# Stage 1's long convolution turned round: input stationary in 32-column tiles, Toeplitz tiles moving; x loaded in two parts, output stored by units

## The chip, the cores and the metric

The kernel runs on one core of a Trainium2 chip. The metric is device time in microseconds of one execution, input load and output store included. The engines are PE (TensorE; PEld is its weight load), DVE (VectorE), ACT (ScalarE), POOL (GpSimd) and SP (SyncE), which here only issues DMAs.

## The reference

A decoder of four layers, each with self attention, cross attention and a feed-forward part, on x of shape (32, 128, 128): 32 sequences, 128 steps, 128 channels, all float32. Every one of the twelve stages ends in `x = layernorm(x + stage(x))`. The stage that the change is in is the first cross attention. Cut to what matters:

```python
# per sequence b: h = layernorm(x) * g + b; sparse attention over ctx (best 32 of 128 keys) gives c
# film = c @ W_film + b_film: scale and shift for the way in and the way out
u  = h * film_in_scale + film_in_shift
# long convolution along the 128 steps, one kernel K[d, :] of 128 taps per channel d
y  = irfft(rfft(u, 2L) * rfft(K, 2L))[:L] + u * D_skip
x1 = x + y * film_out_scale + film_out_shift
out = x + layernorm(x1 + mlp(layernorm(x1))) * g + b
```

## The kernel before

x stays in SBUF as `X` (128 steps on the partitions, 32 sequences, 128 channels) from the first stage to the last. Each stage is a program for all engines, written by hand with semaphores; a stage consists of one or more blocks, and all engines meet at the end of each block. The weights of a stage are fetched while the stage before runs, into one of two large tiles that take turns.

**Start and end.** `load_stage` issues four DMAs from SP in this order: constants, weights of stage 0, x (L365), ctxT (L366). DVE makes small constants and then waits for all of x, and no engine leaves the block before the others. `store_stage` is a block of its own after the last stage: one DMA of X to the output (L400), and a wait for it. In stage 11 (`experts_gelu`) ACT writes X by units of 4 sequences (`block_out`, L4629), each announced by `x_out`.

**Stage 1 (`film_conv`), front block.** Eight units of 4 sequences, on all engines. DVE does the selection of the best 32 keys in four rounds r: `best(u, r, g)` (8 largest, L2838) and `replaced(u, r, g)` (L2855), each for half g of a unit. Between these stand `shifted(u)` (L2873, needs POOL's `root(u)`), `inverse(u-1)` (L2879, needs ACT's sums of exponentials `denominators(u-1)`, L2746), `weights(u-1)` (L2885, needs `inverse`), and `kernel_taps(u)`. POOL's order in a unit u is `root(u)` (L2668, L2671), `chosen(u-1)` (L2681 and L2686, four times; the first waits for `weights(u-1)`), `modulated(u-1)` (L2695 to L2702; L2700 waits for ACT's `film` of L2789 and L2790), then the products for the convolution kernel (L2655, L2660). ACT's `rest(u-1)` (L2758) waits for POOL's L2686 from the third sequence of a unit on, and `exponentials`, `normed` and `filmed` come behind it. The channels' taps gather in `kz`, which SP stores to DRAM (`s4d_kernel`, L2646) once `kernel_sb` is up, some 30 us before the block ends.

**Stage 1, convolution block.** For each channel d the 128 x 128 Toeplitz matrix of its taps is read from `s4d_kernel` by overlapping rows, 16 channels (1024 KB) in a chunk, eight chunks, two buffers: chunk c is issued (L3033) when chunk c-2 has been used. PE does one matmul a channel (L3058): the Toeplitz tile is stationary, and the 32 columns of `UY` (that channel of all 32 sequences) move. DVE (L3047) and ACT (L3039) take turns to copy a chunk's 512 results a partition back into `UY`. All four engines run this as a loop of four steps.

**Stage 1, back block** (L3088 on): SP fetches stage 2's weights; the MLP and the norms follow; its first instruction on DVE reads `UY`.

Matmuls of float32 stand in the trace as two records each, with two weight loads; a transpose as one.

## Time and profile before

| what | value |
|---|---|
| median of 3 runs | 3392.13 us (3390.64 to 3396.54) |
| the profiled execution's own time, and its span | 3384.0 us, 3382.2 us |
| busy over the span: PE, PEld, DVE, ACT, POOL | 82%, 58%, 57%, 41%, 39% |
| granted TensorE clock, mean | 0.889 of full |
| front block of stage 1 | about us 300 to 631.7 |
| convolution block | 631.7 to 693.4 |
| back block | 693.4 to 812 |

The granted clock of TensorE has two levels, 1.2 and 2.4 GHz, shown as 0.50 and 1.00. A row of a timeline has the start, the length, the engine with its line, the operation and, in brackets, how long the engine was idle before and what released it. Busy shares are means over twelve stages with different limits, so what an edit is worth has to be read in its own stretch.

### The profile page before, as it was taken

Reading aid. Unit: us, or ns where it says so; the run is one execution under the profiler, and the core shown is the slowest. Engines: PE = TensorE matmul, PEld = TensorE weight load, DVE = VectorE, ACT = ScalarE, POOL = GpSimd, SP = SyncE. Lnnn points to the kernel's source line nnn. Section 1 sums busy time; section 2 is a strip of 40 time slices with the busy share of each in tenths; the row PEclk is TensorE's granted clock in tenths of the full one; section 3 lists DMA queues with packets and bytes.
Section 4 is the critical chain, followed back from the end, with each engine's and each line's share of the span. In section 5 each row is a group of like instructions: output and inputs, shape, how many; then the busy total and the mean of one; then the engine's idle time right before and its main releaser. Section 6 shows DMA issues by size and latency. Waiting matters only on the chain. (4 is left out here: it accounts for less than half of the span.)

```text
span 3382.2 us, 78574 instructions
## 1 busy us (share of the span) xinstructions
PE 2764.0 (82%) x31778; PEld 1972.8 (58%) x31785; DVE 1936.9 (57%) x5109; ACT 1387.2 (41%) x3112; POOL 1326.2 (39%) x1389
## 2 busy tenths in 40 slices
PE   6992666776665999799899986998789999978985
PEld 3551343654443777566799975666366666655665
DVE  5997998044555344466454444564855555545665
ACT  3552565244344555344322213553143344434554
POOL 3542565154311111444233333453733333324555
PEclk9996777578677999899899997997999999998998
DMA  3000000300000000100000000001000000000000
GB/s 101 3 2 1 1 1 1 87 24 1 1 7 32 1 2 2 40 3 3 8 1 1 1 1 16 2 2 42 4 2 2 2 2 2 2 5 6 2 2 26
DMA packets 24453, 37.29 MB, mean 11 GB/s; under 512 B 568, under 2 KB 21184, under 8 KB 23232
## 3 DMA queue, kind: packets, MB, share of 16 engines
q1 hardware_dynamic: 24096, 32.30, 3.0%
q8 instruction: 253, 4.15, 0.5%
q14 instruction: 104, 0.85, 0.1%
HBM read 30.07 MB, written 2.23 MB: 10 GB/s over the span
## 5 line engine op out<-in xcount | busy, mean ns | idle before, releaser
L1193 POOL TENSOR_TENSOR L_attn__qk<-L_attn__turned 128x512 f32<-128x512 f32 x128 | 161.3, 1271 | 353.0 <-DVE L_attn__turned L1302 353.0
L4247 PE MATMUL psum<-L_ffn__e_hT,weights 128*128 128x256 f32 x1024 | 244.8, 383 | 0.0
L777 DVE TENSOR_REDUCE L_xattn__nm<-psum 128x8 bf16<-128x1024 f32 x128 | 156.4, 1224 | 149.4 <-PE psum L970 143.1
L1302 DVE TENSOR_TENSOR L_attn__turned<-psum,weights 128x1024 f32<-128x1024 f32 x128 | 153.4, 1219 | 144.6 <-PE psum L1409 141.7
L4247 PEld LDWEIGHTS psum<-L_ffn__e_hT,weights 128*128 128x128 f32 x1024 | 186.8, 192 | 20.7
L4101 DVE TENSOR_TENSOR L_ffn__e_a<-L_ffn__e_sg,psum 128x512 f32<-128x512 f32 x128 | 88.0, 687 | 176.5 <-ACT L_ffn__e_sg L4093 176.4
L4093 ACT ACTIVATE L_ffn__e_sg<-psum 128x512 f32<-128x512 f32 x128 | 76.4, 597 | 258.9 <-PE psum L4247 258.9
L717 ACT ACTIVATE L_xattn__pT<-psum 128x1024 f32<-128x1024 f32 x128 | 124.0, 1021 | 59.0 <-PE psum L998 59.0
L4260 PEld LDWEIGHTS psum<-weights,L_ffn__e_a 128*128 128x128 f32 x1024 | 134.4, 191 | 7.2 <-DVE L_ffn__e_a L4101 0.7
L1409 PE MATMUL psum<-L_attn__xT,weights 128*128 128x256 f32 x512 | 136.2, 399 | 2.0 <-DVE L_attn__turned L1302 1.3
L4260 PE MATMUL psum<-weights,L_ffn__e_a 128*128 128x128 f32 x1024 | 135.0, 275 | 0.5 <-DVE L_ffn__e_a L4101 0.5
L1239 ACT ACTIVATE L_attn__qk<-L_attn__qk 128x512 bf16<-128x512 f32 x128 | 77.4, 631 | 87.1 <-POOL L_attn__qk L1193 87.1
L777 DVE TENSOR_REDUCE L_ffn__nm<-psum 128x8 bf16<-128x1024 f32 x64 | 78.2, 1224 | 56.3 <-PE psum L970 56.3
L4020 POOL TENSOR_TENSOR L_ffn__e_half<-L_ffn__e_prod 128x512 f32<-128x512 f32 x32 | 40.6, 1267 | 171.7 <-DVE L_ffn__e_prod L4110 171.7
L712 ACT ACTIVATE L_attn__pT<-L_attn__pT,L_attn__sc 128x1024 f32<-128x1024 f32 x64 | 72.9, 1148 | 79.0 <-DVE L_attn__pT L787 79.0
L1409 PEld LDWEIGHTS psum<-L_attn__xT,weights 128*128 128x128 f32 x512 | 90.4, 192 | 24.1 <-issue 9.7
L2855 DVE MATCH_REPLACE8 L_xattn__front_left<-L_xattn__front_top,L_xattn__front_left 128x128 f32<-128x128 f32 x384 | 101.2, 284 | 0.0
L1627 POOL TENSOR_TENSOR L_xattn__rstd<-L_xattn__mv,eps 128x2 f32<-128x2 f32 x16 | 3.1, 194 | 237.4 <-DVE L_xattn__mv L1749 237.4
L1262 ACT ACTIVATE L_attn__pT<-psum 128x1024 f32<-128x1024 f32 x64 | 62.0, 1021 | 72.7 <-PE psum L1470 72.7
L1311 DVE TENSOR_REDUCE L_attn__nm<-psum 128x8 bf16<-128x1024 f32 x64 | 75.4, 1220 | 26.5 <-PE psum L1440 25.8
L777 DVE TENSOR_REDUCE L_attn__nm<-psum 128x8 bf16<-128x1024 f32 x64 | 77.9, 1220 | 19.1 <-PE psum L970 19.1
L2973 PE MATMUL psum<-L_xattn__front_diag,L_xattn__front_ex 128*128 128x128 f32 x256 | 58.2, 399 | 35.9 <-POOL L_xattn__front_ex L2686 35.9
(669 smaller groups left out, 7649.8 us busy)
## 6 DMA issues: line engine op xcount, KB each, us to landing
L_xattn__toeplitz<-s4d_kernel SPq DMA_DIRECT2D x8, 1024.0 KB, 5.6
weights<-pack SPq DMA_DIRECT2D x1, 3328.0 KB, 11.1
weights<-pack SPq DMA_DIRECT2D x1, 3140.0 KB, 10.4
weights<-pack SPq DMA_DIRECT2D x1, 2370.0 KB, 9.0
out_dram<-X SPq DMA_DIRECT2D x1, 2048.0 KB, 8.7
weights<-pack SPq DMA_DIRECT2D x1, 1732.5 KB, 10.3
ctxT<-ctxT_in SPq DMA_DIRECT2D x1, 1536.0 KB, 21.7
weights<-pack SPq DMA_DIRECT2D x1, 1376.0 KB, 5.8
```

What stands on the lines that cost most here:

```text
L717: nc.scalar.activation(unit, scores[u], ACT.Exp, scale=scale).then_inc(p_sb, 1)
L777: nc.vector.tensor_reduce(nm[:, n % 2, :].rearrange("p (g c) -> p g c", g=4)[:, 2 * u:2 * u + 2, 0:4], scores[u].rearrange("p g (i q) -> p ...
L1193: nc.gpsimd.tensor_tensor(qk[:, p % 2, u], turned[:, g % 2, :, 0:2 * P], turned[:, g % 2, :, 2 * P:4 * P], ALU.add).then_inc(qk_sb, 1)
L1239: nc.scalar.activation(qk16[:, p % 2, u], qk[:, p % 2, u], ACT.Copy).then_inc(qk16_sb, 1)
L1302: nc.vector.tensor_tensor(turned[:, g % 2], proj[u % 2].unsqueeze(1).to_broadcast([P, 2, 4 * P]), k.w(name + "rope").rearrange("p (t q) -> ...
L1311: nc.vector.tensor_reduce(nm[:, n % 2, :].rearrange("p (g c) -> p g c", g=4)[:, 2 * u:2 * u + 2, 0:4], scores[u].rearrange("p g (j q) -> p ...
L1409: last = nc.tensor.matmul(proj[place % 2][:, 2 * P * t:2 * P * t + 2 * P], w[:, P * c:P * c + P], xT[:, p % 2, :], start=True, stop=True)
L2855: last = nc.vector.match_replace(left[:, u % 2, j, h, :], top[:, u % 2, j, h, 8 * r:8 * r + 8], source(u, r, j, h), 2 * NEG)
L4093: nc.scalar.activation(sg[:, g % 2, :], gate[g % 2], ACT.Silu).then_inc(sg_sb, 1)
L4101: nc.vector.tensor_tensor(a[:, g % 2].rearrange("p c s q -> p (c s q)"), sg[:, g % 2, :], up[g % 2], ALU.mult).then_inc(a_sb, 1)
L4247: last = nc.tensor.matmul(bank[g % 2][:, 256 * c:256 * c + 256], k.w(name + w)[:, o:o + P], hT, start=True, stop=True)
L4260: last = nc.tensor.matmul(Y[s][e // 4][:, P * (e % 4):P * (e % 4) + P], a[:, g % 2, c, s, :], k.w(name + "Wd")[:, P * (2 * e + c):P * (2 * ...
```

## The change

Five edits:

1. **Convolution.** The 32 columns of `UY` of a channel become the stationary operand and the Toeplitz tile (128 columns) moves. Four channels at a time use the four 32-column tiles of the array and write to four groups of 32 partitions of one bank. The result stands turned (sequence on the partitions), so ACT copies it to `turned`, PE transposes it back in four transposes a chunk, and DVE copies it into `UY`. The loops are written out.
2. **Chunks.** All eight chunks get their own buffers. The first three go into the weights' tile that is not in use, and are issued in the front block, right after `s4d_kernel` has been stored and POOL's last product has been made. The other five are issued at the start of the convolution block without waits.
3. **DVE's order in the front.** `inverse(u-1)` moves from the end of round 0 to after both halves of `best` in round 1; `weights(u-1)` moves from between these two halves to after `replaced(u, 1, 0)` and `shifted(u)`.
4. **x in two parts.** Sequences 0 to 7, then 8 to 31, with a semaphore each. Stage 0 starts after the first; PE and POOL wait for the second ahead of pair 4.
5. **Output by units.** SP stores each unit of 4 sequences (256 KB) in stage 11 as soon as `x_out` says so; `store_stage` only waits.

```diff
@@ load_stage
-            sp.dma_start(k.X[:], k.x.rearrange("b t d -> t b d")).then_inc(k.x_loaded, 16)
+            xs = k.x.rearrange("b t d -> t b d")
+            sp.dma_start(k.X[:, 0:8, :], xs[:, 0:8, :]).then_inc(k.x_loaded, 16)
+            sp.dma_start(k.X[:, 8:NB, :], xs[:, 8:NB, :]).then_inc(k.x_rest, 16)
             sp.dma_start(k.ctxT[:], k.ctxT_dram).then_inc(k.ctx_loaded, 16)
@@ film_conv, front, SP
                         sp.wait_ge(kernel_stored.sem, 16)
+                        sp.wait_ge(kdiff_sb, COARSE)
+                        for c in range(AHEAD):
+                            sp.dma_start(ahead[:, c], tiles[:, CH * c:CH * c + CH, :]).then_inc(toe_in[c], 16)
@@ film_conv, front, DVE
                                 best(u, r, 0)
+                                best(u, r, 1)
                                 if r == 1 and u >= 1:
-                                    weights(u - 1)
-                                best(u, r, 1)
+                                    inverse(u - 1)
...
                                 replaced(u, r, 0)
                                 if r == 1:
                                     shifted(u)
+                                    if u >= 1:
+                                        weights(u - 1)
                                 replaced(u, r, 1)
-                                if r == 0 and u >= 1:
-                                    inverse(u - 1)
@@ film_conv, convolution block (new)
+                @block.sync
+                    for c in range(AHEAD, CHUNKS):
+                        sp.dma_start(taps_of(c), tiles[:, CH * c:CH * c + CH, :]).then_inc(toe_in[c], 16)
+                @block.scalar
+                    for c in range(CHUNKS):
+                        act.wait_ge(conv_ps, c + 1)
+                        if c >= 2:
+                            act.wait_ge(back_ps, c - 1)
+                        nc.scalar.activation(turned[:, c % 2, :], C_bank[c % 2], ACT.Copy).then_inc(conv_sb, 1)
+                @block.vector
+                    for c in range(CHUNKS):
+                        dve.wait_ge(back_ps, c + 1)
+                        nc.vector.tensor_copy(UY[:, :, CH * c:CH * c + CH],
+                                              T_bank[c % 2].rearrange("p (d b) -> p b d", b=NB)).then_inc(back_sb, 1)
+                @block.tensor
+                    def convolve(c):
+                        pe.wait_ge(toe_in[c], 16)
+                        if c >= 2:
+                            pe.wait_ge(conv_sb, c - 1)
+                        taps = taps_of(c)
+                        for g in range(CH // 4):
+                            for q in range(4):
+                                d = 4 * g + q
+                                last = nc.tensor.matmul(C_bank[c % 2][32 * q:32 * q + 32, P * g:P * g + P],
+                                                        UY[:, :, CH * c + d], taps[:, d, :], start=True, stop=True,
+                                                        skip_group_check=True)
+                        last.then_inc(conv_ps, 1)
+                    def turn_back(c):
+                        pe.wait_ge(conv_sb, c + 1)
+                        if c >= 2:
+                            pe.wait_ge(back_sb, c - 1)
+                        for g in range(CH // 4):
+                            last = nc.tensor.transpose(T_bank[c % 2][:, P * g:P * g + P],
+                                                       turned[:, c % 2, P * g:P * g + P], k.w("ident"))
+                        last.then_inc(back_ps, 1)
+                    convolve(0)
+                    for c in range(CHUNKS):
+                        if c + 1 < CHUNKS:
+                            convolve(c + 1)
+                        turn_back(c)
@@ experts_gelu, SP
-                k.load_weights(sp, k.next_stage(stage))
+                for u in range(UNITS):
+                    sp.wait_ge(x_out, u + 1)
+                    sp.dma_start(k.out.rearrange("b t d -> t b d")[:, 4 * u:4 * u + 4, :],
+                                 k.X[:, 4 * u:4 * u + 4, :]).then_inc(k.stored, 16)
```

Stage 11 had no next stage, so the line removed there issued nothing. In stage 0, `if stage == 0 and p == 4` puts a wait for `x_rest` ahead of POOL's `with_bias(4)` and PE's transposes of pair 4.

## Rows read from the trace of the kernel before

**Rows 1.** The convolution: busy time of engines, granted clock, DMA share, GB/s:

```profile
632.00:693.40 61.40, 54.81 (x256) 54.69 (x256) 2.77 (x4) 2.39 (x4) 0.00 (x0) 0.50 0.48 137
```

**Rows 2.** PE and ACT over the convolution, in order of time:

```profile
637.84 54.81 PE L3058 MATMUL psum<-L_xattn__UY,L_xattn__toeplitz 128*128 x256 [6.77 <-DMA L_xattn__toeplitz<-s4d_kernel]
692.79 0.60 ACT L3039 ACTIVATE L_xattn__UY<-psum 128x512 f32 x1 [13.06 <-PE psum L3058]
```

**Rows 3.** The timeline of SP's queue, us 590 to 700:

```profile
599.22 0.34 SPq L2646 DMA_DIRECT2D s4d_kernel<-L_xattn__kz  x1
631.96 47.44 SPq L3033 DMA_DIRECT2D L_xattn__toeplitz<-s4d_kernel  x8
```

**Rows 4.** The Toeplitz transfers issued in us 600 to 660:

```profile
DMA to landing us min/median/max: 5.4/5.6/8.8
```

**Rows 5.** PE's timeline in stage 0, 32-column tiles, and one window's clock:

```profile
45.04 1.94 PE L1012 MATMUL psum<-L_attn__pT,L_attn__vz 128*32 128x128 f32 x32
52.70 1.08 PE L1012 MATMUL psum<-L_attn__pT,L_attn__vz 128*32 128x128 f32 x32
...
45.04:46.98 1.94, 1.94 (x42) 1.47 (x40) 1.23 (x1) 1.45 (x2) 0.00 (x0) 0.50 0.00 0
```

**Rows 6.** PE's timeline in the front of stage 1, full array:

```profile
484.73 1.06 PE L2924 MATMUL psum<-consts,X 128*128 128x128 f32 x4
495.80 2.04 PE L2973 MATMUL psum<-L_xattn__front_diag,L_xattn__front_ex 128*128 128x128 f32 x8 [0.87 <-POOL L_xattn__front_ex L2686]
```

**Rows 7.** The timeline of SP's queue at the start:

```profile
1.79 0.83 SPq L365 DMA_DIRECT2D X<-x_in  x1
2.67 10.94 SPq L366 DMA_DIRECT2D ctxT<-ctxT_in  x1
```

**Rows 8.** The timeline of POOL at the start of stage 0:

```profile
18.06 0.31 POOL L611 MEMSET L_attn__nm<- 128x256 bf16 x1 [15.44 <-POOLq L359]
```

**Rows 9.** DMA issues: KB each, us from issue to landing:

```profile
out_dram<-X SPq DMA_DIRECT2D x1, 2048.0 KB, 8.7
weights<-pack SPq DMA_DIRECT2D x1, 321.5 KB, 2.9
s4d_kernel<-L_xattn__kz SPq DMA_DIRECT2D x1, 128.0 KB, 2.1
X<-x_in SPq DMA_DIRECT2D x1, 0.5 KB, 15.7
```

**Rows 10.** The timeline at the end:

```profile
3373.10 0.39 SPq L400 DMA_DIRECT2D out_dram<-X  x1
```

**Rows 11.** Timelines of ACT, DVE and POOL in unit 6 of the front:

```profile
517.05 0.38 ACT L2790 ACTIVATE L_xattn__FO<-psum 128x256 f32<-128x256 f32 x1
...
522.32 0.25 DVE L2879 RECIPROCAL L_xattn__front_den<-L_xattn__front_den 128x16 f32<-128x16 f32 x1 [2.97 <-ACT L_xattn__front_etop L2746]
524.05 0.76 DVE L2885 TENSOR_TENSOR L_xattn__front_den<-L_xattn__front_den,L_xattn__text_gate 128x16 f32<-128x16 f32 x1
...
527.51 1.02 POOL L2671 TENSOR_TENSOR L_xattn__front_rstd<-L_xattn__front_rstd,neg_half 128x4 f32<-128x4 f32 x1
528.50 1.04 POOL L2681 TENSOR_TENSOR L_xattn__front_diag<-consts,L_xattn__front_den 128x512 f32<-128x512 f32 x1
```

**Rows 12.** Timelines of DVE and POOL, units 0 and 1 of the front:

```profile
317.22 0.17 DVE L2873 SCALAR_TENSOR_TENSOR L_xattn__front_shift<-L_xattn__front_mv,L_xattn__front_rstd 128x4 f32<-128x4 f32 x1
...
349.96 0.92 DVE L2873 SCALAR_TENSOR_TENSOR L_xattn__front_shift<-L_xattn__front_mv,L_xattn__front_rstd 128x4 f32<-128x4 f32 x1
...
340.52 1.01 POOL L2671 TENSOR_TENSOR L_xattn__front_rstd<-L_xattn__front_rstd,neg_half 128x4 f32<-128x4 f32 x1
346.38 1.04 POOL L2681 TENSOR_TENSOR L_xattn__front_diag<-consts,L_xattn__front_den 128x512 f32<-128x512 f32 x1 [4.85 <-DVE L_xattn__front_den L2885]
```

**Rows 13.** Waits in the front: engine, line, releaser; total us, times, longest:

```profile
DVE L_xattn__front_den L2879 <- ACT L_xattn__front_etop L2746: 23.5, 6, 13.4
POOL L_xattn__front_diag L2681 <- DVE L_xattn__front_den L2885: 7.5, 2, 4.9
```

More of the change, by code:

```diff
@@ L399, in _ @@
         def _(sp):
-            sp.dma_start(k.out.rearrange("b t d -> t b d"), k.X[:]).then_inc(k.stored, 16)
-            sp.wait_ge(k.stored, 16)
+            if 11 in STAGES:
+                sp.wait_ge(k.stored, 16 * (NB // 4))
+            else:
+                sp.dma_start(k.out.rearrange("b t d -> t b d"), k.X[:]).then_inc(k.stored, 16)
+                sp.wait_ge(k.stored, 16)
 def rms_root(k, pool, ms, s, t, mean_square, plus_eps, root):
@@ L563, in with_bias @@
                 def with_bias(p):
+                    if stage == 0 and p == 4:
+                        pool.wait_ge(k.x_rest, 16)
                     if p >= 2:
@@ L902, in turn @@
                         pe.wait_ge(xT_sb, p)
+                    if stage == 0 and p == 4:
+                        pe.wait_ge(k.x_rest, 16)
                     for s in range(2):
@@ L2450, in film_conv @@
         kernel_stored = sig.one("kernel_stored", 16, 1)
+        CH, AHEAD = 16, 3
+        CHUNKS = P // CH
+        tiles = bass.AP(tensor=kernel_dram, offset=0, ap=[[1, P], [2 * P, P], [1, P]])
+        toe_in = [sig.one(f"toeplitz_loaded{c}", 16, 1).sem for c in range(CHUNKS)]
+        ahead = k.weights[1 - BUFFER[stage]][:, 0:AHEAD * CH * P].rearrange("p (c d l) -> p c d l", c=AHEAD, d=CH)
         with ExitStack() as mid:
@@ L3017, in film_conv, with sb, event, taps_of @@
         with ExitStack() as ctx:
-            CH = 16
-            toeplitz = ctx.enter_context(nc.sbuf_tensor(f"{name}_toeplitz", [P, 2, CH, P], F32))
-            toe_in = sig.pair("toeplitz_loaded", 16)
-            conv_ps, conv_sb = sig.pair("conv_ps"), sig.pair("conv_sb")
-            tiles = bass.AP(tensor=kernel_dram, offset=0, ap=[[1, P], [2 * P, P], [1, P]])
+            def sb(what, shape, dt=F32):
+                return ctx.enter_context(nc.sbuf_tensor(f"{name}_conv_{what}", shape, dt))
+            def event(what):
+                return sig.one("conv_" + what, 1, 1).sem
+            toeplitz = sb("toeplitz", [P, CHUNKS - AHEAD, CH, P])
+            turned = sb("turned", [P, 2, 4 * P])
+            C_bank, T_bank = k.bank[0:2], k.bank[2:4]
+            conv_ps, conv_sb, back_ps, back_sb = event("ps"), event("sb"), event("back_ps"), event("back_sb")
+            def taps_of(c):
+                return ahead[:, c] if c < AHEAD else toeplitz[:, c - AHEAD]
             with nc.Block() as block:
@@ L3028, in _ @@
                 def _(sp):
-                    for c in range(P // CH):
-                        s, turn_of = c % 2, c // 2
-                        if turn_of:
-                            sp.wait_ge(conv_ps[s].sem, turn_of)
-                        sp.dma_start(toeplitz[:, s], tiles[:, CH * c:CH * c + CH, :]).then_inc(toe_in[s].sem, 16)
+                    for c in range(AHEAD, CHUNKS):
+                        sp.dma_start(taps_of(c), tiles[:, CH * c:CH * c + CH, :]).then_inc(toe_in[c], 16)
@@ L3035, in _ @@
                 @block.scalar
                 def _(act):
-                    with act.Fori(0, P // (2 * CH)) as t:
-                        act.wait_ge(conv_ps[1].sem, conv_ps[1].at(t, 1))
-                        nc.scalar.activation(UY[:, :, bass.ds(2 * CH * t + CH, CH)],
-                                             k.bank[5][:].rearrange("p (d b) -> p b d", b=NB),
-                                             ACT.Copy).then_inc(conv_sb[1].sem, 1)
+                    for c in range(CHUNKS):
[3 more added lines that the diff above has]
+                        nc.scalar.activation(turned[:, c % 2, :], C_bank[c % 2], ACT.Copy).then_inc(conv_sb, 1)
@@ L3051, in _ @@
                 @block.tensor
                 def _(pe):
-                    with pe.Fori(0, P // (2 * CH)) as t:
-                        for s in range(2):
-                            pe.wait_ge(toe_in[s].sem, toe_in[s].at(t, 16))
-                            pe.wait_ge(conv_sb[s].sem, conv_sb[s].at(t, 0))
-                            for j in range(CH):
-                                last = nc.tensor.matmul(k.bank[4 * s + 1][:, NB * j:NB * j + NB], toeplitz[:, s, j, :],
-                                                        UY[:, :, bass.ds(2 * CH * t + (CH * s + j), 1)], start=True,
-                                                        stop=True)
-                            last.then_inc(conv_ps[s].sem, 1)
+                    def convolve(c):
[10 more added lines that the diff above has]
+                        last.then_inc(conv_ps, 1)
```

8 lines of the change are left out of this document (3 added, 5 removed).

## The prediction, made before the changed kernel was run

> **What bounds the kernel now.** I read the page first, only to see that no single engine bounds it: PE is busy 82% of the span, DVE 57%, and these are means over twelve stages. An edit is therefore worth what it is worth in its own stretch, and I went to five: the start, the front of stage 1, its convolution, the block behind it and the end.
>
> In the convolution PE itself is the limit: 54.8 us busy out of 61.4, at half clock (0.50) all the while, with the DMA share below half [rows 1]. The reader should see the order of time as well: PE waits 6.8 us for its first chunk, then never again, and ACT's last copy ends at 692.79 + 0.60 = 693.4 [rows 2]. SP's queue is empty between 599.22 and 631.96, when the chunks are issued [rows 3]. At the start every engine stands until 18.06 [rows 8], because x, issued at 1.79, lands 15.7 us later, at 17.5 [rows 7, 9]. At the end one store of 2048 KB takes 8.7 us with nothing beside it [rows 9, 10].
>
> The front needs the most care, since the edit of DVE's order is made there. DVE looks like the victim of a wait: it waits 23.5 us in six places for ACT's sums before `inverse` [rows 13]. But follow unit 6. ACT's film ends at 517.4; POOL then adds the film, makes the products and the root, and ends the root at 527.51 + 1.02 = 528.53. Its `chosen` starts at 528.50, at once. DVE had finished `weights` at 524.05 + 0.76 = 524.8, 3.7 us earlier [rows 11]. POOL waited for DVE there in two units only, 7.5 us together [rows 13]: the second (unit 1) and the last. So the round trip POOL, ACT, PE, ACT, POOL sets the pace of the front, DVE follows it, and DVE's wait is slack.
>
> **The change part by part.**
>
> *Convolution.* The same form of matmul, a 32-column tile with 128 float32 columns moving, stands in stage 0: 32 records took 1.94 us at half clock (0.50) and 1.08 us in a later instance, which I take for the full level [rows 5]. A chunk is 16 channels of two records, so 32 records, against 54.8 / 8 = 6.85 us now [rows 1]. Four full transposes are added to each chunk, 1.06 us [rows 6]. A chunk then costs PE 2.1 to 3.0 us, eight cost 17 to 24. The copies (0.60 us each on ACT [rows 2], about as much on DVE) run beside it, and only the last shows.
>
> The rate of chunks is the other limit. Of the two issued together at 631.96 the first landed after 5.6 us, at 637.6, the later one 8.8 us after its own issue, some 0.36 us later, so at 641.1 [rows 3, 4]: 3.5 us a chunk. Three chunks are fetched in the empty time of the queue, from about 601.4 (599.22 + 2.1 [rows 3, 9]): 5.6 + 2 x 3.5 = 12.6 us, there by 614. The waits put on SP are met: nothing else is queued on it, and POOL's last product is long made. The other five are issued at 631.96 and the last lands at 637.6 + 4 x 3.5 = 651.6. PE starts it at 651.8 (it started 0.2 us after landing before [rows 2]); + 1.08 for the chunk, + 0.60 for ACT's copy, under which the transposes of chunk 6 lie, + 1.06, + 0.7 for DVE's copy and 0.3 for hand-overs = 655.5. Saved: 693.4 - 655.5 = 37.9 us. If PE stays at half clock, it is the bound from 632.1 on: 24 + 0.7 = 656.8, saved 36.6. I take 37.9, since two limits meet at nearly the same time.
>
> One rule speaks against this price. The Trainium skill, "TensorE: Matmul & The Clock Gate", Part 3, The mechanism, says that a weight load overlaps a running matmul only where their row groups differ, and four column tiles all use every row. By its figure of columns / 1.2 ns, 27 ns for 32 columns, an estimate is 0.86 us more for 32 records, on the path once, behind the last landing: 37.0 saved. The trace speaks against it, because rows 5 have 32 loads and 32 matmuls in 1.08 us.
>
> *DVE's order.* What it adds is told by POOL's first instruction of `chosen(u-1)`. Before, `weights(u-1)` was ready before the root in units 2 to 7. Now it stands behind `shifted(u)`, which needs the very root that POOL does just ahead of `chosen`. So POOL ends the root, DVE does `shifted` (0.17 us when POOL is idle [rows 12]) and `weights` (about the same), and only then POOL goes on: about 0.45 us with hand-overs, six times = 2.7 us. If the two ran as long as they do beside a busy POOL (0.92 and 0.76 [rows 11, 12]) it would be 1.8, six times = 10.8. I take 0.45, as POOL is waiting, not working. Behind it on POOL stand all of `chosen` and `modulated`; ACT's `rest`, `exponentials` and film wait for these, and so the loop that sets the pace. Unit 1 is dearer: DVE is late there, POOL already waits until 346.38 with its root done at 341.5, and `shifted` comes at 349.96 [rows 12]. `weights` will come right behind it, at about 350.15, and POOL starts at 350.4: + 4.1. The last `weights` keeps its place. The removed wait (23.5 - 13.4 = 10.1 us in five places [rows 13]) only moves to `shifted`, where DVE now waits for the root. Sum: + 6.8 us, bounds + 14.9 (4.1 + 10.8) and, if DVE did set the pace, - 10.1.
>
> *x in two parts.* The last three quarters of x, 1536 KB, take 5.3 us at 3.5 us per 1024 KB, so sequences 0 to 7 are there by 12.2 instead of 17.5. But nobody leaves the block before SP, and SP sits in the issue of ctxT until 2.67 + 10.94 = 13.6 [rows 7]; the order and bytes in the queue stay the same. The block ended 0.57 us after the last event before (17.5 to 18.06). New start: 14.2, - 3.9 us. Bounds: - 5.3, if SP gets free as early as x, and 0, if it is held until all of x is down. The waits for the rest, ahead of pair 4, cost nothing: in 17.5 us it is down, while stage 0 is at its first pairs. On SP one more issue of 0.8 us lies under the blocked one.
>
> *Output by units.* Seven stores lie under the work of the units behind them. The last one, 256 KB, lies between 128 KB in 2.1 us and 321.5 KB in 2.9 us [rows 9]; I take 2.7 for 8.7: - 6.0 us, bounds - 6.6 and - 5.8.
>
> *Elsewhere* nothing moves: the back block's weights are fetched in its own block as before, and the tile borrowed for three chunks is free by then.
>
> **Sum.** - 37.9 + 6.8 - 3.9 - 6.0 = - 41.0 us. The profiled execution took 3384.0 us around a span of 3382.2, so it would take 3343.0. It was 8.1 us quicker than the median of the runs, which I take for a property of the profiled execution and not of the work. Predicted median: 3392.1 - 41.0 = 3351.1 us. Differences under 0.2%, 6.8 us, I count as none.
>
> **The rivals.**
>
> *The front pays nothing, or gains.* If units overlap so that POOL's later start is made good by an earlier DVE, the 6.8 go away: 3344.3. If DVE's waits were the pace, 10.1 us come off as well: 3334.2. For it: in unit 1 DVE is late, and POOL waits 4.85 us for it [rows 12]. Against it: POOL's 3.7 us of distance in unit 6, and only two waits of POOL for DVE.
>
> *The change doesn't do what it says: the three early chunks don't come early*, because SP is held at one of its waits until the block's end. Then eight chunks follow each other from 631.96: 637.6 + 7 x 3.5 = 662.1, + 3.9 for the same tail = 666.0, saved 27.4, time 3361.6. Against it: 30 us of empty queue. The same time comes out if transfers run at two thirds of the rate measured.
>
> *The column tiles don't run beside each other in the array*, and the kernel is slower. Each record then costs what one in the full array costs, 2.04 / 8 = 0.255 us [rows 6]: 8.2 us a chunk, 9.2 with the transposes, 632.1 + 8 x 9.2 + 0.7 = 706.4, + 13.0 for the convolution in place of - 37.9, in all + 9.9: 3402.0. It decides the sign from about 7.8 us a chunk of matmuls: (61.4 + 9.7 - 0.8) / 8 - 1.06. Against it: 1.94 at half clock for the same count [rows 5]. What is new is that the weights are read with a stride of 512 bytes.
>
> **How the numbers follow.** The forecast (chunks set the pace, the front pays) has 0.50; the front paying nothing or gaining 0.27; chunks late or slow 0.15; tiles one after another 0.04; 0.04 for several small misses that leave 10 us or less. The likeliest case alone has 3346 to 3360, from its bounds. The range reaches from the front with most of its gain to late chunks with the front's price a little higher: 3336 to 3366. Only the third rival, and part of the last case, are not faster: faster 0.94, same 0.02, slower 0.04.
>
> **What would show it.** In the profile after: stage 0 starts at about 14 instead of 18.06; in SP's queue three Toeplitz issues at about 601 and five at the start of the block; PE's groups of 32 records in 1.1 to 1.9 us, and waits of PE for DMA between the later chunks; the convolution block about 23.5 us long; DVE's wait at `inverse` gone and one at `shifted` in its place; POOL waiting for `weights` in every unit, 4 us in unit 1 and about half a microsecond in the others; the last store under 3 us. The prediction is wrong if POOL's waits are nearly nil, if the front gets shorter, if PE's granted clock in the front shifts (the five units from 346.38 to 528.50 took 36.4 us each [rows 11, 12], and 3% of that, over six units, is already the price that I put on the front), or if PE doesn't reach the pace of the transfers.

## The result, and the profile after

The changed kernel took 3347.56 us (median of 4 runs, 3341.05 to 3352.58) beside 3392.94 us for the kernel before on the same chip (4 runs, 3390.64 to 3396.54): ratio 0.9869, interval 0.9854 to 0.9884, that is 44.5 us less (39 to 50). A second timing of the same two kernels gave 3352.83 us beside 3391.37: ratio 0.9881, interval 0.9866 to 0.9896. The two medians lie 3.5 us under and 1.7 us over the predicted 3351.1.

The span of the profiled execution went from 3382.2 to 3343.4 us. I cut both at the same instructions:

| stretch | before, us | after, us | difference | predicted |
|---|---|---|---|---|
| start, until POOL's first record of stage 0 | 18.06 | 14.14 | -3.9 | -3.9 |
| stage 0, until the root of unit 0 of the front | 289.9 | 288.4 | -1.5 | 0 |
| to the root of unit 1 | 32.5 | 32.5 | 0 | 0 |
| front: root of unit 1 to the convolution's Toeplitz issue | 291.4 | 299.3 | +7.9 | +6.8 |
| convolution: that issue to the first record of the block behind | 61.7 | 25.1 | -36.6 | -37.9 |
| that block and stages 2 to 11, until the last write of X starts | 2677.5 | 2679.6 | +2.1 | 0 |
| from there to the end of the span | 11.0 | 4.4 | -6.6 | -6.0 |
| sum | 3382.2 | 3343.4 | -38.8 | -41.0 |

**The convolution.** PE's timeline of the changed kernel over the block (start, duration, in brackets the idle time before it and what ended it), which answers to [rows 2]:

```profile
634.43 3.73 PE L3084 MATMUL psum<-weights,L_xattn__UY 128*32 128x128 f32 x64 [0.94 <-PEq L2658]
638.09 1.11 PE L3094 MATMUL psum<-consts,L_xattn__conv_turned 128*128 128x128 f32 x4
639.14 1.41 PE L3084 MATMUL psum<-weights,L_xattn__UY 128*32 128x128 f32 x32
...
641.06 1.26 PE L3084 MATMUL psum<-L_xattn__conv_toeplitz,L_xattn__UY 128*32 128x128 f32 x32
642.25 0.66 PE L3094 MATMUL psum<-consts,L_xattn__conv_turned 128*128 128x128 f32 x4
643.68 1.25 PE L3084 MATMUL psum<-L_xattn__conv_toeplitz,L_xattn__UY 128*32 128x128 f32 x32 [0.77 <-DMA L_xattn__conv_toeplitz<-s4d_kernel]
...
648.44 1.25 PE L3084 MATMUL psum<-L_xattn__conv_toeplitz,L_xattn__UY 128*32 128x128 f32 x32 [2.92 <-DMA L_xattn__conv_toeplitz<-s4d_kernel]
...
652.05 2.02 PE L3084 MATMUL psum<-L_xattn__conv_toeplitz,L_xattn__UY 128*32 128x128 f32 x32 [1.51 <-DMA L_xattn__conv_toeplitz<-s4d_kernel]
...
655.29 1.80 PE L3084 MATMUL psum<-L_xattn__conv_toeplitz,L_xattn__UY 128*32 128x128 f32 x32 [0.17 <-DMA L_xattn__conv_toeplitz<-s4d_kernel]
657.02 1.41 PE L3094 MATMUL psum<-consts,L_xattn__conv_turned 128*128 128x128 f32 x8
```

The first four chunks find their tiles there, and the last four wait for a transfer (the very last for 0.17 us only): transfers bound the end of the block, not PE. Read the durations too: 1.87 us for 32 records in the first pair, 1.25 in the middle, 2.02 near the end. The granted clock of the same stretches goes with them (columns: window, length, busy time and count on PE, weight loads, DVE, ACT, POOL, then the granted clock, DMA share and GB/s):

```profile
634.40:638.20 3.80, 3.77 (x65) 3.41 (x66) 0.00 (x0) 0.62 (x1) 0.00 (x0) 0.50 0.67 190
639.10:644.90 5.80, 5.03 (x106) 4.13 (x105) 2.08 (x3) 1.36 (x2) 0.00 (x0) 0.95 1.15 301
644.90:648.40 3.50, 0.62 (x6) 0.38 (x4) 0.69 (x1) 0.60 (x1) 0.00 (x0) 1.00 1.19 292
652.00:655.30 3.30, 3.08 (x38) 2.29 (x38) 0.14 (x1) 0.60 (x1) 0.00 (x0) 0.50 0.56 137
```

The granted clock is at the half level (0.50) at first and nearly at the full one (0.95) after. While PE stands idle for the transfers, from 645.5 to 648.4, it is still 1.00, and it is 0.50 under the chunk that starts at 652.05.

**SP's queue** answers to [rows 3 and 7]; the first four lines are the start, the others the surroundings of the convolution:

```profile
1.63 0.43 SPq L367 DMA_DIRECT2D X<-x_in  x1
2.28 3.66 SPq L368 DMA_DIRECT2D X<-x_in  x1
5.98 7.75 SPq L369 DMA_DIRECT2D ctxT<-ctxT_in  x1
14.14 0.35 SPq L350 DMA_DIRECT2D weights<-pack  x1
...
605.75 0.34 SPq L2663 DMA_DIRECT2D s4d_kernel<-L_xattn__kz  x1
608.03 5.45 SPq L2667 DMA_DIRECT2D weights<-s4d_kernel  x3
634.39 13.67 SPq L3057 DMA_DIRECT2D L_xattn__conv_toeplitz<-s4d_kernel  x5
```

SP is free of ctxT's issue at 5.98 + 7.75 = 13.73, and stage 0 starts 0.4 us later, at 14.14, as was worked out. The three early chunks are issued 26 us before the block, and have landed before it starts.

**The front.** POOL's and DVE's waits in the front of the changed kernel (engine, line, releaser; us in total, times, longest), beside [rows 13]:

```profile
POOL L_xattn__front_xg L2720 <- ACT L_xattn__FO L2810: 117.6, 8, 16.9
POOL L_xattn__front_diag L2701 <- DVE L_xattn__front_den L2905: 13.6, 8, 8.7
...
DVE L_xattn__front_shift L2893 <- POOL L_xattn__front_rstd L2691: 23.7, 6, 4.2
DVE L_xattn__front_den L2899 <- ACT L_xattn__front_etop L2766: 20.5, 7, 15.0
```

POOL now waits for the weights in every unit, 13.6 us instead of 7.5. DVE waits 23.7 us at `shifted` for POOL, where it did not wait before. Its wait at `inverse` is not gone: the one of the last unit is still there (13.4 us before, 15.0 now), and of the other 10.1 us 5.5 are left, in six places. So DVE stands idle some 20 us more in all; the price is what POOL waits, not this. The hand-over in unit 3, on POOL and DVE:

```profile
420.40 1.02 POOL L2691 TENSOR_TENSOR L_xattn__front_rstd<-L_xattn__front_rstd,neg_half 128x4 f32<-128x4 f32 x1
421.78 1.04 POOL L2701 TENSOR_TENSOR L_xattn__front_diag<-consts,L_xattn__front_den 128x512 f32<-128x512 f32 x1 [0.37 <-DVE L_xattn__front_den L2905]
...
421.45 0.16 DVE L2893 SCALAR_TENSOR_TENSOR L_xattn__front_shift<-L_xattn__front_mv,L_xattn__front_rstd 128x4 f32<-128x4 f32 x1 [3.91 <-POOL L_xattn__front_rstd L2691]
421.53 0.17 DVE L2905 TENSOR_TENSOR L_xattn__front_den<-L_xattn__front_den,L_xattn__text_gate 128x16 f32<-128x16 f32 x1
```

POOL's root ends at 421.42, `shifted` starts at 421.45, `weights` follows, and POOL's `chosen` starts at 421.78.

**The end.** The last write of X, whose four records end at 3340.69, then nothing but the last store (2.7 us to the end of the span, 3343.4):

```profile
3339.04 1.65 ACT L4673 ACTIVATE X<-L_ffn__r,L_ffn__shift,L_ffn__rstd 128x128 f32<-128x128 f32 x4 [4.21 <-DVE L_ffn__shift L4753]
```

### The profile page after: what moved, and what is told of

The parts are those of the page before. It is cut to its first block and busy times, and to the rows that moved or that the text cites. A ratio compares the mean times of both kernels' runs of the same rounds, so it can differ in the third digit from the quotient of the medians.

```text
span 3343.4 us, 78491 instructions
## 1 busy us (share of the span) xinstructions
PE 2724.1 (81%) x31810; PEld 1931.3 (58%) x31817; DVE 1930.9 (58%) x5113; ACT 1390.3 (42%) x3116; POOL 1326.8 (40%) x1389
## 5 line engine op out<-in xcount | busy, mean ns | idle before, releaser
L722 ACT ACTIVATE L_attn__pT<-L_attn__pT,L_attn__sc 128x1024 f32<-128x1024 f32 x64 | 72.9, 1149 | 79.1 <-DVE L_attn__pT L797 79.1
## 6 DMA issues: line engine op xcount, KB each, us to landing
weights<-pack SPq DMA_DIRECT2D x1, 3328.0 KB, 10.5
```

## The experiments

Each kernel is the changed one with one edit, unless it says otherwise. Ratios are against the kernel before, run on the same chip; its own median lay between 3388.17 and 3392.94 us from timing to timing, so kernels of different timings are compared by their ratios. "Front" below is the stretch from the root of unit 1 to the first Toeplitz issue of the convolution block, and "later stages" is that from the block behind the convolution to the last write of X.

### The old order of DVE's operations

```
 best(u, r, 0)
-best(u, r, 1)
 if r == 1 and u >= 1:
-    inverse(u - 1)
+    weights(u - 1)
+best(u, r, 1)
...
 shifted(u)
-if u >= 1:
-    weights(u - 1)
 replaced(u, r, 1)
+if r == 0 and u >= 1:
+    inverse(u - 1)
```

> The changed kernel with DVE's order in the front of stage 1 put back (inverse at the end of round 0, weights between the two halves of best in round 1). My theory: the loop through POOL and ACT sets the pace, so POOL's new waits (3.8 us more in unit 1, 0.37 us in six units) go away and the span falls by 6.1 us from 3343.4 to about 3337, give or take 5 for the granted clock; POOL waits for weights in two units only, as before. Rival: DVE's wait for the sums is what costs, then taking the new order away makes the front 10 us longer, span 3353.

Measured: 3347.4 us, ratio 0.9884 (0.9865 to 0.9903). In the trace POOL waits for weights in two units again (4.86 and 2.69 us), and the front takes 289.8 us instead of 299.3: 9.5 us less. But the later stages took 2689.7 us instead of 2679.6, the span is 3342.4 us where some 3337 were expected, and the ratio, beside 0.9869, shows no gain. The place of the price is confirmed, its worth for the whole kernel is not; it was run again further down.

### The new order alone, in the kernel before

The same edit in the other direction, made to the kernel before.

> The kernel before with only the new order of the VectorE operations. Theory: the wait of GpSimd for the weights of unit 0 grows from 4.9 to 8.7 us, and in the six later units one of 0.4 us appears; from the second root to the first Toeplitz issue of the convolution it takes 297 to 300 us instead of 291.4, so the kernel is 5 to 9 us slower than before. Rival: the order costs only the 3.8 us of unit 1, and the rest of the changed kernel's 7.9 us came from its other parts (the Toeplitz chunks fetched ahead, granted clock): 295 us, 4 us slower.

Measured: 3398.70 us beside 3390.33 (12 and 17 runs), ratio 1.0020 (1.0009 to 1.0031): 6.8 us slower (3 to 10.5). POOL's waits for weights are the 13.6 us in 8 places of the changed kernel:

```profile
POOL L_xattn__front_diag L2681 <- DVE L_xattn__front_den L2885: 13.6, 8, 8.7
```

The front took 296.2 us in the profiled execution, 4.8 more than before. That is between what the two theories gave, and the median is in the range of both. What is settled: with this order alone the kernel before is slower, and the waits are all there. Where the 6.8 us lie is not settled: in this profiled execution the later stages took 2687.3 us against 2677.5, which is more than the front lost.

### The products one place earlier on POOL

If POOL sets the pace, then work that stands between the film and `chosen` on POOL should come off when it is moved under POOL's wait for the film.

```
 pool.wait_ge(u2_sb, u + 1)
+if u + 2 < COARSE:
+    kernel_products(u + 2)
 pool.wait_ge(film_sb, 4 * u + 4)
...
 if u == 0:
     kernel_products(0)
-if u + 1 < COARSE:
-    kernel_products(u + 1)
+    kernel_products(1)
```

> The changed kernel with POOL's products for the convolution kernel (7.1 us a unit) moved to where POOL waits for ACT's film, so that they no longer stand between the film and the next root. My theory, that the loop over POOL sets the pace: the loop loses 7.1 of its 37.9 us, and DVE, busy some 33.5 us a unit, becomes the pace, so 4 us in each of six units go, about 24 us, span about 3320 (3317 to 3328). Rival, DVE or ACT with PE set the pace: nothing changes, span 3340 to 3346.

Measured: 3332.47 us, ratio 0.9832 (0.9813 to 0.9851). The front took 288.6 us, 10.7 less than in the changed kernel, where 24 were expected. The waits say where the rest went:

```profile
POOL L_xattn__front_xg L2722 <- ACT L_xattn__FO L2811: 75.3, 8, 16.3
POOL L_xattn__front_diag L2701 <- DVE L_xattn__front_den L2906: 32.6, 8, 8.7
```

POOL's wait for the film fell by 42 us, and 19 us of that came back as a wait for DVE's weights, 3.5 us in each of the six middle units, which was 0.37 before. So POOL's work between the film and `chosen` did lie on the loop that sets the pace (POOL itself is busy for only 22 us of a unit), and 7 us a unit taken off it bring up the next limits. Which they are, the units show (a unit counted from POOL's first `chosen` to the next one; columns as above). The first two lines are this run, the third is a unit of the kernel with the early weights, described next:

```profile
452.15:489.87 37.72, 25.16 (x108) 14.40 (x107) 32.95 (x222) 21.84 (x83) 22.24 (x18) 0.73 0.00 1
489.87:523.87 34.00, 22.76 (x108) 13.43 (x107) 32.84 (x222) 21.85 (x83) 22.25 (x18) 0.80 0.00 1
444.39:478.39 34.00, 22.77 (x105) 13.49 (x106) 34.00 (x222) 21.78 (x84) 22.25 (x17) 0.80 0.00 1
```

Four of the six units took 34.0 to 35.3 us. The other two kept 37.7: the granted clock in them is 0.73, and DVE waits for PE. In a unit of 34.0 us DVE is busy for 32.8 and waits 1.2 for ACT's sums, while POOL waits for DVE; in the third line DVE is busy for all of the 34.0, and is the limit. And in this run the stretch behind the last `chosen` took 32.8 us against 28.7 in the changed kernel's, which no part of the edit explains.

### The old order and the early products together

The two edits above, and, in the second kernel, `inverse(0)` and `weights(0)` moved right behind `statistics(1)`:

```
 statistics(u)
+if r == 0 and u == 1:
+    inverse(0)
+    weights(0)
```

> The old order with the kernel products early, without the early weights of unit 0. If the early weights in unit 1 made the 12.9 us by which the mixed kernel's front was shorter than that of the early products alone, this front takes some 284 us or more; if the old order did it together with the early products, it takes 279 to 281 us (the mixed kernel's 275.7 plus the 4 to 5 us of unit 1).

> The changed kernel with three edits to the front: the old order of the VectorE operations back, the kernel products of the next unit moved ahead of the film add on GpSimd, and, in unit 1 alone, the inverse and the weights of unit 0 right after the statistics of unit 1. Theory (GpSimd's chain sets the front until VectorE's own 33 us a unit do): the first diagonal product of unit 1 starts 10 us after the second root instead of 4 us later still, the wait for the first weights falls from 4.9 to under 1 us, the periods of the units are the 34.0 us (or 37.6 us at the lower granted clock) of the run with the products early, and the stretch from the second root to the first Toeplitz issue of the late block is some 284 us instead of 299; the median some 12 to 16 us under the changed kernel. Rival: VectorE is the limit already in both, and the old order gives nothing on top of the early products: 288 us for the stretch, and the median of the run with the early products alone.

Measured: without the early weights of unit 0 3336.13 us, ratio 0.9828 (0.9814 to 0.9842), front 284.1 us; with them 3331.18 us, ratio 0.9827 (0.9808 to 0.9846), front 275.7 us. Between the front of the early products alone (288.6) and that of the mix lie 12.9 us, 4.5 of them on the step to the old order and 8.4 on the step to the early weights; the first theory had some 284 us or more for the kernel between. Of these, POOL's wait in unit 1 accounts for 3.8 and 4.9 us (8.68, then 4.86, then nothing); the rest is within what fronts of one order vary. On POOL, unit 1 of the mix starts `chosen` straight behind the root, where it waited 8.68 us in the changed kernel:

```profile
336.89 1.01 POOL L2691 TENSOR_TENSOR L_xattn__front_rstd<-L_xattn__front_rstd,neg_half 128x4 f32<-128x4 f32 x1
337.86 1.04 POOL L2701 TENSOR_TENSOR L_xattn__front_diag<-consts,L_xattn__front_den 128x512 f32<-128x512 f32 x1
```

The ratios of all three kernels with early products lie within 0.0005 of each other, so what the front gains on top of the early products isn't resolved by the timings. Each of the three is some 0.4 to 0.5% under the changed kernel: of the two timed side by side, 0.9828 (0.9814 to 0.9842) against 0.9881 (0.9866 to 0.9896).

### All chunks issued in the block

```
-sp.wait_ge(kdiff_sb, COARSE)
-for c in range(AHEAD):
-    sp.dma_start(ahead[:, c], ...)
...
-for c in range(AHEAD, CHUNKS):
+for c in range(CHUNKS):
```

> The changed kernel with all eight Toeplitz chunks issued at the start of the convolution block, none in the front. If the pace of the chunks bounds the block (3.5 us each), the block grows by three chunks, 10.5 us, from 25.0 to about 35.5, span about 3354. Rival, PE bounds it and the early fetch only hides the first landing: the block grows by no more than the wait for the first chunk, 5 to 6 us, span about 3349.

Measured: 3362.2 us, ratio 0.9922 (0.9901 to 0.9943). SP's queue and a part of PE's timeline:

```profile
631.99 5.50 SPq L3054 DMA_DIRECT2D weights<-s4d_kernel  x3
637.53 19.01 SPq L3054 DMA_DIRECT2D L_xattn__conv_toeplitz<-s4d_kernel  x5
667.70 0.35 SPq L350 DMA_DIRECT2D weights<-pack  x1
...
637.86 2.00 PE L3081 MATMUL psum<-weights,L_xattn__UY 128*32 128x128 f32 x32 [6.75 <-DMA weights<-s4d_kernel]
641.47 2.01 PE L3081 MATMUL psum<-weights,L_xattn__UY 128*32 128x128 f32 x32 [1.61 <-DMA weights<-s4d_kernel]
...
656.92 2.02 PE L3081 MATMUL psum<-L_xattn__conv_toeplitz,L_xattn__UY 128*32 128x128 f32 x32 [0.55 <-DMA L_xattn__conv_toeplitz<-s4d_kernel]
...
660.53 2.01 PE L3081 MATMUL psum<-L_xattn__conv_toeplitz,L_xattn__UY 128*32 128x128 f32 x32 [0.55 <-DMA L_xattn__conv_toeplitz<-s4d_kernel]
```

PE waits for every chunk; most follow each other at 3.6 us (641.47 - 637.86, 660.53 - 656.92). From the first issue at 631.99 to the next block's first record at 667.75 it is 35.8 us, against 25.1: +10.7, where the theory said +10.5 and the rival +5 to 6. Three chunks fetched ahead are three times the transfer's rate, 3 x 3.6 = 10.8. The timing agrees: the ratio is 0.0041 to 0.0053 above the changed kernel's two, 14 to 18 us, uncertain by 9. PE's records took the 2.0 us of the half level for seven of the eight chunks, which cost nothing, since transfers were the bound.

### The column tiles in turn

Same matmuls, same tiles, another order: all four groups of one tile, then the next tile.

```
-for g in range(CH // 4):
-    for q in range(4):
+for q in range(4):
+    for g in range(CH // 4):
```

> The changed kernel with the two loops of the convolution's matmuls exchanged: four matmuls in a row use the same 32-column tile before the next tile is used, same work and same result. If neighbours overlap only because they are on different column tiles, a record costs 0.14 us at full clock to 0.255 at half, 4.5 to 8.2 us a chunk instead of 1.25, and the convolution block takes 42 to 75 us instead of 25, span 3360 to 3393. Rival, tiles overlap whatever the order of issue: 25 us, no change.

Measured: 3357.95 us, ratio 0.9902 (0.9880 to 0.9924). PE's timeline and a window:

```profile
643.94 2.57 PE L3084 MATMUL psum<-weights,L_xattn__UY 128*32 128x128 f32 x32
...
659.36 2.56 PE L3084 MATMUL psum<-L_xattn__conv_toeplitz,L_xattn__UY 128*32 128x128 f32 x32
...
650.00:662.00 12.00, 12.00 (x143) 10.69 (x142) 2.77 (x4) 2.06 (x5) 0.00 (x0) 1.00 0.58 142
```

At the full level (1.00) 32 records take 2.57 us where the changed kernel's took 1.25 at 0.95: twice as long. So neighbouring records overlap when they go to different column tiles, and the order is what brings it. Whether it is the matmuls or the weight loads that no longer overlap isn't separated, and the order in which channels are read changed with it. The expected 42 to 75 us for the block were missed by far, for two reasons: a tile served several times running costs 0.08 us a record, not the expected 0.14 to 0.255, and PE came up to the full level. A chunk with its transposes then takes 3.08 us (643.94 to 647.02 in PE's timeline), still less than the transfers' 3.6, so with three chunks ahead PE never waits and bounds the block itself. It took 27.65 us against 25.1. From the third chunk on PE's clock is 1.00 here, where PE never waits; with all chunks issued in the block, where it waits for each, it is 0.50 up to the last chunk.

### x in one load again

```
-sp.dma_start(k.X[:, 0:8, :], xs[:, 0:8, :]).then_inc(k.x_loaded, 16)
-sp.dma_start(k.X[:, 8:NB, :], xs[:, 8:NB, :]).then_inc(k.x_rest, 16)
+sp.dma_start(k.X[:], xs).then_inc(k.x_loaded, 16)
```

> The changed kernel with x loaded in one transfer again. Theory: stage 0 starts at 18.0 instead of 14.1 us, and nothing later depends on it: the second root of the front comes 3.9 us later. Rival: the two parts also made stage 0 itself 1.5 us shorter, so the second root comes 5.4 us later. Either way the median is 4 to 5 us over the changed kernel.

Measured: 3356.08 us, ratio 0.9901 (0.9875 to 0.9927). ctxT's issue and the start of stage 0:

```profile
2.68 11.14 SPq L368 DMA_DIRECT2D ctxT<-ctxT_in  x1
...
18.38 0.31 POOL L616 MEMSET L_attn__nm<- 128x256 bf16 x1 [15.75 <-POOLq L360]
```

SP gets out of ctxT's issue at 13.82, as with two loads (13.73), and the start is at 18.38: now x's landing is last, with two loads it is SP. From the start of stage 0 to the root of unit 1 it took 323.0 us, against 321.0 and 323.1 in the two profiles of the changed kernel (so its second root is 6.3 us later than in the one and 4.1 later than in the other). One profile against one can't tell 3.9 from 5.4. But stage 0 alone took 290.5 us here, and 287.2 to 290.7 in the ten profiles with two loads, so nothing speaks for the rival, and the 1.5 us of stage 0 in the table need no cause in the two loads. The start itself, 18.38 against 13.9 to 14.2, is clear. The ratio is 0.0020 to 0.0032 above the changed kernel's two, 7 to 11 us, uncertain by 10, so it holds the expected 4 to 5.

### One store again

The eight stores of the last stage are replaced by the one behind it.

> The changed kernel with the output stored by one transfer at the end. Theory: from the end of the last write of X to the end of the span 9.4 us instead of 2.7, and the median 6.6 us over the changed kernel. Rival: the eight stores cost something on the way (they share the queue and the ports with stage 11), so that without them stage 11 is 1 to 3 us shorter and the loss is only 4 to 5 us.

Measured: 3350.78 us, ratio 0.9877 (0.9856 to 0.9898). In the trace the last write of X and the store behind it:

```profile
3351.74 1.65 ACT L4671 ACTIVATE X<-L_ffn__r,L_ffn__shift,L_ffn__rstd 128x128 f32<-128x128 f32 x4 [4.22 <-DVE L_ffn__shift L4751]
...
3353.64 0.39 SPq L406 DMA_DIRECT2D out_dram<-X  x1
```

From the end of the write, 3353.39, to the end of the span, 3362.7, it is 9.3 us, against 2.7. Whether the stores cost something on their way is seen in stage 11 itself, since the later stages as a whole vary by more than the rival's 1 to 3 us: from the first to the last of the 32 writes of X it took 79.3 us here, and 79.1 to 79.3 in the ten profiles with eight stores. So these profiles show no cost of the stores. The median doesn't show the 6.6 us: its ratio lies between the two of the changed kernel. The price is read from the trace, and this timing neither confirms nor refutes it.

### The changed kernel and the old order once more, side by side

> The changed kernel once more, beside the next two on one chip, because the first timing of the old order showed none of the 9.5 us that its trace showed in the front. Both theories: 0.987 of the kernel before, front stretch (second root to the issue of the five Toeplitz chunks) 297 to 301 us.

> The changed kernel with the old order of the VectorE operations. Theory: the 9.5 us of the front are real and the first timing only lay high by the scatter of the later stages (2677.5 to 2690.6 us for identical code): 6 to 10 us faster than the changed kernel beside it. Rival: what the front gives is taken back behind it (stages 2 to 11 take 10 us longer whenever the front ends early): the median is that of the changed kernel within 2 us, and the profile shows some 2689 us for stages 2 to 11 again.

Measured: 3352.83 us (4 runs) for the changed kernel and 3354.19 us (4 runs) for the old order, ratios 0.9881 and 0.9893 (0.9878 to 0.9908). The fronts took 298.8 and 292.2 us, so 6.6 us are gained there; the later stages took 2686.3 and 2689.8, so 3.5 are lost again. The loss can be placed. From the first record of the block behind the convolution to SP's next weights issue, with the same work in both windows (the changed kernel, then the old order):

```profile
662.03:914.70 252.67, 164.29 (x821) 114.06 (x821) 127.37 (x532) 112.81 (x246) 112.62 (x134) 0.76 0.01 4
653.76:910.30 256.54, 168.64 (x821) 117.83 (x821) 127.62 (x533) 113.16 (x246) 112.61 (x134) 0.75 0.01 4
```

That is 3.9 us, at a granted clock that is 0.01 lower, and from there to the end the two take the same time within half a microsecond. The first profile of the old order has 256.5 us in the same stretch too. Of the six profiles of the changed kernel and its variants with the new order (the early products apart) five have 252.7 or 252.8; the tiles in turn have 257.3. So in both traces something of the front's gain is given back right behind it, but it is 3.9 of 6.6 us here, not all.

The rest isn't explained. The old order's profiled span is 4.8 us shorter (3347.9 against 3352.7), yet its median is 1.4 us longer. The profiled execution was the quickest of the four with the old order and the slowest of the four with the new one, so it doesn't stand for the timings. The timings, by the intervals of both pairs, leave room for a gain of up to 3 us and speak against more. The mean granted clock over the timed runs is lower with the old order in both pairs (0.8935 and 0.8915 against 0.8975 and 0.8955). But that doesn't place the loss: 0.8948 was also measured in two kernels with the new order, and in the side-by-side profiles the clock is lower ahead of the convolution too (stage 0 0.91 against 0.92, the front 0.70 against 0.71). The rival's two numbers came, the median within 2 us and some 2689 us for the later stages. Its reason did not: beside the changed kernel of the same timing they are 3.5 us longer and not 10, and the other 6.5 us and more, by which six profiles lie above the changed kernel's first one, come in both orders.

Over the thirteen profiles the later stages took some 2677.5 to 2679.6, 2686.1 to 2687.7, or 2689.7 to 2690.6 us, at mean granted clocks of 0.920 to 0.922, 0.918 or 0.919, and 0.917 or 0.918. The two profiles with the old order alone in the changed kernel fell in the last group, and so did the tiles in turn; the kernel before, with the same old order, is in the first, and with the new order in the second. What chooses the group was not found.

## Why the prediction was right

*What bounds the kernel.* The reading that PE at half clock bounded the convolution and transfers would bound it next is borne out: PE waits for DMA ahead of each of the last four chunks, and taking the early fetch away costs three chunks' transfers, 10.7 us.

*The convolution, -37.9.* It is -36.6. The block took 25.1 us instead of 23.5 (before, the table's 61.7 us hold 0.3 us behind ACT's last copy). Two errors make it up: the last chunk started 20.9 us after the five were issued, not 19.8, because one gap between chunks was 4.76 us (643.68 to 648.44) and not 3.5; and the tail from the last chunk's start to the next block took 4.2 us instead of 3.7. In the tail the last chunk's records took 1.80 us instead of the 1.08 of [rows 5]: PE's clock had fallen to the half level behind the waits and came back while they ran. The four transposes took 0.66 us at the full level instead of the 1.06 of the half level in [rows 6], which gave half of it back. Even at the full level the 32 records take 1.25 us here and not 1.08; no run shows why. That the case of PE at half clock throughout had been priced at the same 36.6 is a coincidence.

*That tiles run beside each other.* Right, and under a condition that the prediction didn't name. It took the price of 32 records from stage 0 [rows 5] by the form of the matmul; the form alone would have given 2.5 us as well, in the other order of the loops. The rival in which tiles don't overlap took the price of the full array, 0.255 us a record; measured for tiles in turn is 0.08 us at the full clock, so this rival's mechanism exists, and its price was too high by far. Its limit of 7.8 us a chunk, which was to decide the sign, holds only if the 6.8 us that count as no difference are added: the other terms take off 9.9 us and the front adds 6.8, so a block 3.1 us longer than before already evens out, (61.4 + 3.1 - 0.8) / 8 - 1.06 = 6.9. In the order used, the Trainium skill's rule ("TensorE: Matmul & The Clock Gate", Part 3, The mechanism) that a weight load overlaps only a matmul in another row group isn't what this trace shows: the loads of all four tiles use every row, and 32 loads and 32 matmuls took 1.25 us, against 2.57 with each tile served four times running.

*DVE's order, +6.8.* The front grew by 7.9 us. The wait in unit 1 grew by 3.83 us (predicted 4.1); the six others are 0.37 us of wait each, 2.2 us (predicted 2.7, at 0.45). That is 6.1. The waits are paid in full, as middle units of the same granted clock show (columns as above; two units of the kernel before, then two of the changed one, each from POOL's first `chosen` to the next):

```profile
491.16:528.50 37.34, 24.88 (x105) 14.89 (x106) 34.37 (x222) 21.74 (x84) 22.14 (x18) 0.73 0.00 1
454.19:491.16 36.97, 22.81 (x105) 13.13 (x106) 34.39 (x222) 21.56 (x83) 22.09 (x18) 0.82 0.00 1
...
421.78:459.36 37.58, 24.93 (x105) 14.94 (x106) 32.95 (x222) 21.88 (x84) 22.17 (x18) 0.73 0.00 1
459.36:496.71 37.35, 22.82 (x105) 13.14 (x106) 32.93 (x222) 21.77 (x84) 22.11 (x18) 0.82 0.00 1
```

The new order is 0.2 us longer at 0.73 and 0.4 at 0.82. That the front of this one profile came so near the forecast is in part luck: its seven units took 8.1 us more than before, of which the waits are 2.2, and the stretch behind the last `chosen` 4.1 us less (28.7 against 32.8), though that stretch takes 28.6 to 28.7 or 32.0 to 32.8 us in either order. All profiles together are the better witness: three fronts with the old order took 289.8 to 292.2 us, seven with the new one 295.3 to 302.5, and the means are 7.2 us apart. The granted clock over them, whose shift was named as a sign of being wrong, was 0.70 to 0.72 in the old order and 0.70 to 0.74 in the new.

The step "POOL is waiting, so `shifted` and `weights` cost their short durations" held: 0.16 and 0.17 us. DVE's wait was slack, as argued: DVE stands idle some 20 us more than before, and it is POOL's 6.1 us that count. One sign did not come: the wait at `inverse` is halved, not gone. What the prediction did not see is that the term hardly counts in the changed kernel's median: undone there, the ratio stays where it is within its interval, while in the kernel before the same edit costs 6.8 us. A lower granted clock right behind the front takes 3.9 us back; the rest is open. The sum came out right with this term in it, but the two timings could not have told it from zero.

*x in two parts, -3.9.* As predicted, and by the mechanism given: SP's blocked issue of ctxT ends at 13.7, and the first part of x landed 10.5 us after its issue, at 12.2. With ctxT's issue out of the way the start could be some 1.5 us earlier still, an estimate from these two times; that was not tried.

*Output by units, -6.0.* It is -6.65: the last 256 KB took 2.3 us from issue to landing, where 2.7 were taken. Seven stores lie under stage 11, at no cost that the profiles show.

*The span's other parts, 0.* Stage 0 and the later stages moved by -1.5 and +2.1 us. Over all profiles stage 0 took 287.1 to 290.7 us, and the later stages 2677.5 to 2690.6, so these are within the scatter of identical code. That scatter, 13 us, is larger than the 3.5 and 1.7 us by which the medians missed the forecast: the terms are shown one by one, the closeness of the sum is in part luck. The prediction corrected for the profiled execution being 8.1 us quicker than the median; the changed kernel's profiled execution was 2.4 us quicker than its median in the first timing and 1.6 us slower in the second. The offset was indeed the execution's own.

## What to carry to other kernels

When an engine's long wait is to be removed, ask whose work ends the wait, and look at that engine's own next wait: if it is nil, the wait is slack, and operations that now stand behind the pacing engine's own work make it late. Moving 7 us a unit of the pacing engine's work under its own wait was the only edit to the front that the timings resolve in the changed kernel, and even so the front gained 10.7 us of the expected 24 before the next limits came up.

Matmuls in narrow column tiles gain from overlap only when neighbours in the instruction stream go to different tiles; put the loop over tiles innermost. Where transfers of a fixed rate bound a short block, a chunk fetched in an idle stretch of the queue is worth its share of the rate: 10.7 us for three chunks of 3.6.

And when a gain in one stage is to be checked, identical code behind it must be looked at too: here it varied by 13 us, more than most of the terms. Compare it at the same instructions, not at the same distance in time.

## What the runs showed of the hardware

- The same 32-column float32 matmuls took 1.25 us for 32 when they went round the four tiles and 2.57 us when each tile was served four times running.
- PE, busy for 54.81 of 61.4 us, had a granted clock of 0.50 through the whole block before [rows 1]. In the changed block, with less to do, the window from 639.1 on shows 0.95, and in the one with tiles in turn 1.00. Why the full array's matmuls stayed at the half level and the column tiles' did not was not tried. Where the tiles waited for every chunk, the clock was 0.50 until the last one.
- Issues on SP took long when several large transfers were under way: the issues of five chunks of 1024 KB took 13.7 us in all, those of eight in a row 24.5 us, and ctxT's issue took 7.75 us behind x in two parts, 10.9 to 11.1 behind x in one.
- Identical code in the later stages took one of three groups of durations up to 13 us apart, with a mean granted clock of 0.922 at the one end and 0.917 at the other.
